# The inverse of the softmax sums sent over the partitions once per head group and applied as the context sums leave PSUM

## The reference, cut to what matters

```
xn = layernorm(ctx) * gamma_media + beta_media        # 722 media rows a batch
ln = layernorm(x + attn) * gamma_lat + beta_lat       # 100 latent rows
q  = (ln @ Wq + bq) * 128 ** -0.5                     # 8 heads of 128
k, v = split(concat([xn, ln]) @ Wkv + bkv)
out = softmax(q @ k.T) @ v                            # over 822 keys
x  = x + out @ Wo + bo
```

## Time and profile before

| | |
|---|---|
| median of three runs | 1082.91 us (1082.25 to 1085.74) |
| profiled execution | 1084.0 us, its span 1082.3 us |
| granted TensorE clock, mean | 0.975 of full speed |
| TensorE busy | 1011.3 us, 93% of the span |
| VectorE busy | 795.0 us, 73% |
| ScalarE busy | 580.2 us, 54% |
| GpSimd busy | 119.4 us, 11% |
| recurrence / units / last unit / tail / experts | 0 to 168 / 168 to 640 / 640 to 698 / 698 to 816 / 818 to 1082 us |

### The profile page before, as it was taken

One profiled execution on the slowest core, in us unless ns is written; L12 is line 12 of the kernel. 1 busy time (PEld: TensorE's weight loads), 2 busy tenths in 40 slices (PEclk: granted clock), 3 DMA queues, 4 the chain that ended last, 5 costly groups with the idle time before them and its releaser, 6 DMA issues.

```text
span 1082.3 us, 14817 instructions
## 1 busy us (share of the span) xinstructions
PE 1011.3 (93%) x5274; PEld 925.5 (86%) x5275; DVE 795.0 (73%) x1052; ACT 580.2 (54%) x770; POOL 119.4 (11%) x100
## 2 busy tenths in 40 slices
PE   8999998799999999999999997977798999999997
PEld 6969998798999999999999996966676888888886
DVE  6888456888878787888878655764567984956992
ACT  4426564545546464554646543641435864856881
POOL 3615001000000000000000000000012111111221
PEclk9999999899999999999999998998798999999999
DMA  9333877531525326252442138387555992975970
GB/s 262 124 109 125 304 266 243 129 114 47 167 79 138 131 61 177 66 168 75 132 141 47 61 48 279 109 262 260 125 163 158 344 364 68 353 251 176 363 285 22
DMA packets 119854, 183.88 MB, mean 170 GB/s; under 512 B 38945, under 2 KB 61985, under 8 KB 119795
## 3 DMA queue, kind: packets, MB, share of 16 engines
q1 hardware_dynamic: 118114, 178.55, 52.7%
q0 software_dynamic: 1680, 4.54, 1.2%
HBM read 146.94 MB, written 37.11 MB: 170 GB/s over the span
## 4 chain that ended last, share of the span: by engine, by line
PE 60%; DVE 15%; DMA 10%; ACT 6%; SPq 5%; issue 4%; POOL 0%; DVEq 0%; POOLq 0%; ACTq 0%
PE bank L587 17%; PE bank L588 16%; PE bank L589 16%; DMA xt_l<-scr_keys 4%; ACT xn_h L1457 2%; DVE z_l L1739 2%; DMA scr_rows<-mvr 2%; ACT z_h L1523 2%; PE bank L1334 2%; DVE str__65 L1721 1%; SPq L694 1%; PE bank L1072 1%; DMA w<-in_WoT 1%; PE bank L1074 1%; PE bank L1073 1%
## 5 line engine op out<-in xcount | busy, mean ns | idle before, releaser
L1739 DVE TENSOR_TENSOR wsl<-stage,wsh 128x2048 fp32r<-128x2048 f32 x63 | 143.7, 2291 | 23.1 <-ACT wsh L1528 18.1
L587 PE MATMUL bank<-ph,xn_h 128*128 128x400 f32 x384 | 140.2, 365 | 1.6 <-DVE pl L1739 1.6
L587 PE MATMUL bank<-qt_h,xt_h 128*128 128x400 f32 x384 | 134.8, 351 | 7.3 <-DMA xt_l<-scr_keys 7.3
L588 PE MATMUL bank<-pl,xn_h 128*128 128x400 f32 x384 | 133.3, 347 | 0.0
L588 PE MATMUL bank<-qt_l,xt_h 128*128 128x400 f32 x384 | 132.6, 345 | 0.0
L589 PE MATMUL bank<-ph,xn_l 128*128 128x400 f32 x384 | 132.5, 345 | 0.0
L589 PE MATMUL bank<-qt_h,xt_l 128*128 128x400 f32 x384 | 132.1, 344 | 0.0
L1528 ACT CAST wsh<-stage 128x2048 fp32r<-128x2048 f32 x63 | 120.4, 1918 | 10.6 <-PE bank L589 9.0
L1472 ACT ACTIVATE pa<-bank,rsr 128x400 f32<-128x400 f32 x96 | 56.4, 592 | 75.7 <-PE bank L589 72.3
L1498 ACT COPY zf<-bank 128x400 f32<-128x400 f32 x64 | 31.6, 494 | 101.7 <-PE bank L1190 101.4
L587 PEld LDWEIGHTS bank<-qt_h,xt_h 128*128 128x128 f32 x384 | 72.9, 190 | 9.0 <-issue 8.8
(11 more groups left out here) (277 smaller groups left out, 2330.3 us busy)
## 6 DMA issues: line engine op xcount, KB each, us to landing
stage<-in_W SPq DMA_DIRECT2D x63, 1024.0 KB, 6.1
scr_q<-st SPq DMA_DIRECT2D x16, 800.0 KB, 6.7
qf<-scr_q SPq DMA_DIRECT2D x16, 800.0 KB, 7.5
scr_z<-zf SPq DMA_DIRECT2D x16, 800.0 KB, 5.2
zr<-scr_z SPq DMA_DIRECT2D x16, 800.0 KB, 6.6
rt<-in_ctxT SPq DMA_DIRECT2D x7, 1444.0 KB, 13.2
raw<-in_ctx SPq DMA_DIRECT2D x8, 768.0 KB, 4.6
raw<-in_ctx SPq DMA_DIRECT2D x8, 512.0 KB
```

What stands on the lines that cost most here:

```text
L587: pe.matmul(dest, lh, rh, start=start and k == 0, stop=False)
L588: pe.matmul(dest, lh, rl, start=False, stop=False)
L1739: return dve.tensor_tensor(dst, src, high.bitcast(F32), ALU.subtract)
```

## The change

In place of dividing the heads' outputs in the tail, the context sums are divided as they leave PSUM:

- After each unit's reciprocal SyncE stores the 100x4 inverses to DRAM, waits for the landing, and loads them back as `inv`, 400 columns laid over the 128 partitions (`spread_inverse`, two DMAs per unit, one buffer).
- VectorE evacuates each context piece by a product with `inv` (`weighted`, 64 of them), ScalarE adds beta to it in place (`add_shift`, 64), which replaces `context_out`. The bank comes free after `weighted`.
- In the tail `ivt`, `cb`, `bmx`, `normalised` and the events `v` go. `V` has 400 columns; `ot_h` and `ot_l` read the bank.
- The first units' and the last unit's work is in another order on all engines, and SyncE issues the latent keys before the raw rows and the queries.

```
+            def spread_inverse(u):
+                b, g = divmod(u, 2)
+                sp.wait_ge(s_inv, u + 1)
+                sp.dma_start(d_iv[u].rearrange("(h t) -> t h", h=GH), iv[0:T, b, g * GH:(g + 1) * GH],
+                             allow_slow_non_contiguous=True).then_inc(s_ivd, 16)
+                sp.wait_ge(s_ivd, 16 * (u + 1))
+                sp.wait_ge(s_zn, ND * u)
+                sp.dma_start(inv[:], bc(d_iv[u], GR)).then_inc(s_ivl, 16)
...
+            def weighted(u, dc):
+                b, g = divmod(u, 2)
+                dve.wait_ge(s_zb, ND * u + dc + 1)
+                if dc == 0:
+                    dve.wait_ge(s_ivl, 16 * u + 16)
+                    if b:
+                        dve.wait_ge(s_zd[g], 16 * b)
+                dve.tensor_tensor(zf[g][:, :, dc, :], context_bank(u, dc)[:, 0:GR].rearrange("p (h t) -> p h t", h=GH),
+                                  inv[:].rearrange("p (h t) -> p h t", h=GH), ALU.mult).then_inc(s_zn, 1)
...
-                act.copy(zf[g][:, :, dc, :], zbank[n % 2][:, 0:GR].rearrange("p (h t) -> p h t", h=GH)).then_inc(s_zn, 1)
+            def add_shift(u, dc):
+                act.wait_ge(s_zn, ND * u + dc + 1)
+                at = zf[u % 2][:, :, dc, :]
+                act.activation(at, at, ACT.Identity, bias=gbm[:, 1, dc:dc + 1]).then_inc(s_zbeta, 1)
...
             def spread_sums(u):
-                pe.wait_ge(s_p, NP * (u + 1))
+                pe.wait_ge(s_sum, u + 1)
...
+            def context_bank(u, dc):
+                return bank[dc] if u == NU - 1 and dc >= 2 else zbank[dc % 2]
...
-                            pe.wait_ge(s_on, k - 3)
+                            pe.wait_ge(s_otl, ot_done(k - 4))
+                        elif k == 2:
+                            pe.wait_ge(s_zn, ND * NU)
...
                     elif what == "C":
+                        pe.wait_ge(s_zn, ND * NU)
...
-                        act.activation(ot_h[:, h, OVER:], ivt[k % NIV][:], ACT.Identity, bias=cb[:, h:h + 1]
+                        act.activation(ot_h[:, h, OVER:], bank[k % 4][:, 0:HT], ACT.Identity, bias=bv[:, h:h + 1]
...
-                    inverse(0)
+                    queries(1, 0)
                     for half in range(2):
                         keys_centred(1, half)
+                    inverse(0)
```

More of the change, by code:

```diff
@@ L221, in build @@
     x1b = [mem(f"x1b{k}", [P, D]) for k in range(2)]
-    dg = mem.over(x1b[0], "dg", [P, GR])
+    dg, inv = (mem.over(t, name, [P, GR]) for t, name in zip(x1b, ("dg", "inv")))
     tables_at = mem.where(pa[0]) + 4 * 4 * FC * 4
@@ L242, in build @@
     zn = HALF * ND * T
-    z_at = [(raw, 0), (raw, zn), (xt_h, HEADS * D + 64), (qt_h, -32), (xn_h, 2 * HEADS * HT - 32), (ph[0], 0)]
+    z_at = [(raw, 0), (raw, zn), (xt_h, HEADS * D + 64), (qt_h, 0), (xn_h, 2 * HEADS * HT), (ph[0], 0)]
     zr = [mem.over(t, f"zr{k}", [P, HALF, ND, T], skip=n) for k, (t, n) in enumerate(z_at)]
     z_l = [mem.over(t, f"z_l{k}", [P, HALF, ND, T], F32R, skip=n) for k, (t, n) in enumerate(z_at)]
[L246 to L252, removed]
+    z_h = [mem.over(qt_h, f"z_h{k}", [P, HALF, ND, T], F32R, skip=(k + 1) * zn) for k in range(3)]
+    z_h.append(mem.over(pa[0], "z_h3", [P, HALF, ND, T], F32R))
     UNITS = 2 * HEADS
@@ L266, in build @@
     ot_l = mem.over(xt_l, "ot_l", [P, HEADS, OVER + HT], F32R, skip=ot_skip + ot_n)
-    assert mem.where(xt_l) + ot_skip * 4 >= zr2_end + HT * 4
+    assert mem.where(xt_l) + ot_skip * 4 >= mem.where(xt_h) + (HEADS * D + 64 + HALF * ND * T) * 4
     mem.at = tail_at
@@ L1273, in _ @@
                 if u == 1:
+                    context(0, 0)
                     spread_sums(0)
-                if u < NU - 1:
+                    context(0, 1)
+                    turn_maxima(1)
+                    context(0, 2)
+                    spread_maxima(1)
+                    context(0, 3)
+                elif u < NU - 1:
                     context(u - 1, 0)
@@ L1279, in _ @@
                     spread_maxima(u)
+                    context(u - 1, 2)
+                    context(u - 1, 3)
                 else:
@@ L1282, in _ @@
                     context(u - 1, 1, lambda: spread_maxima(u))
-                context(u - 1, 2)
-                context(u - 1, 3)
+                    context(u - 1, 2)
+                    context(u - 1, 3)
             context(NU - 1, 0)
-            context(NU - 1, 1)
             spread_sums(NU - 1)
-            context(NU - 1, 2)
-            context(NU - 1, 3)
+            for dc in range(1, ND):
+                context(NU - 1, dc)
             finish(tail)
@@ L1608, in _ @@
                 if u == 1:
-                    evacuate(1, 0)
-                    queries(1, 0)
-                    for c in range(1, 5):
+                    for c in range(4):
                         evacuate(1, c)
@@ L2179, in _ @@
                     rows_norm(b + 1, 1)
-            weights(NU - 1)
-            values_low(3)
-            inverse(NU - 1)
+            u = NU - 1
+            shifts(u)
+            weighted(u - 1, 0)
+            for part in range(NP):
+                shift(u, part)
+            weighted(u - 1, 1)
+            first_sum(u)
+            weighted(u - 1, 2)
+            second_sum(u)
+            weights_low(u, 0)
+            weights_low(u, 1)
+            last_sum(u)
+            weights_low(u, 2)
+            weighted(u - 1, 3)
+            inverse(u)
+            for k in range(ND):
+                values_low(k)
             low_unit(0)
             low_unit(1)
+            weighted(u, 0)
+            weighted(u, 1)
             low_unit(2)
@@ L2187, in _ @@
             output_low(1)
+            weighted(u, 2)
             low_unit(3)
+            weighted(u, 3)
             output_low(2)
```

207 lines of the change are left out of this document (81 added, 126 removed), and 8 rows, old and new, of the table tail.

## The result

| | before | changed |
|---|---|---|
| median of the runs | 1082.58 us | 1133.43 us |
| profiled execution, span | 1082.3 us | 1130.1 us |
| granted TensorE clock, mean | 0.975 | 0.956 |

The ratio is 1.0484 (95% interval 1.0428 to 1.054): 4.8% slower. The direction was forecast, the size was not: 1096 us was predicted, and 1133 lies outside the 1080 to 1115 of the prediction's own case. (The kernel before has one more run here than in the table ahead of the prediction, hence 1082.58 for 1082.91.)

A forecast was written before the change was run, and what follows sets the result against it. TensorE was taken to bound the softmax units and a chain the tail, with a new DRAM round trip paid in each unit. 8 - 7 + 29 + 10 - 27 = +13 gave 1096 us, range 1064 to 1148.

The forecast's parts named there:

- the prediction's own case: Whole kernel: new store lands in 6.3 us, 1096 us in all, range 1080 to 1115; chance 0.42.
- Odd units: Six units, u = 3 to 13: `dg` 1.3 us late each, +8, less 7 for `xt_l`.
- a price per piece: New store of inverses: landing time above `rec`'s 2.7 us goes with the number of pieces, 400 against 768, giving 6.3 us.
- the -7 for `xt_l`: Odd units: latent keys put ahead of raw rows on SyncE remove TensorE's 7.3 us of waits for `xt_l`.
- Even units: Seven units, u = 2 to 14: spread 3.1 us late and 1.6 of clock, +29 in all; bounds 0 and +54.
- its idle fifth: VectorE over the units: 36 us of `weighted` products, 2.3 us a unit, fit its idle time and cost nothing.
- my two bounds: Even units: store lands at 501.3 if not hindered, 505.9 if it starts after the large transfers; middle 503.6 taken.
- First units: Piece 2 of unit 0's context waits 8.1 us for the inverse, 1.6 of clock: +10, bounds +6 and +13.
- Last unit: Unit 15 to `V` 1: earlier casts offset by waiting for `weighted(15,3)`, about 698 to 700; nothing counted.
- Tail: Heads follow every 2.6 us, then 2.4, where one took 4.68: -27, bounds -12 and -35.
- (b): Rival: the store doesn't get cheaper with fewer pieces, 9.6 us, 1153 us; 8 us gives 1125; chance 0.26.
- (a): Rival: adjacent elements cost nothing, the store lands in 2.7 us, 1061 us; chance 0.18.

The follow-up runs named there:

- e7: Kernel before with six test stores of inverses added, differing in number, size and spacing of pieces, each alone on the queue; ran once, 1093.35 us.
- e5: Kernel before with only SyncE's order changed, latent keys issued ahead of raw rows and queries; 1078.0 us, ratio 0.998 to the kernel before.
- e1: Changed kernel without the trip: no store or load of the inverses, `inv` set to one; 1108.9 us, ratio 1.025 to the kernel before.
- e2: Changed kernel with the inverses stored in 100 pieces of 16 bytes for 400 of 4, `inv` read with a stride; 1065.5 us, ratio 0.987.
- e4: Changed kernel with the raw rows issued ahead of the load of the inverses in odd units; 1194.2 us, ratio 1.105 to the kernel before.
- e3: Changed kernel, even units: store of the inverses issued ahead of `zf` and `qf`, load behind them; 1135.5 us, ratio 1.052 to the kernel before.
- e9: Changed kernel, 4-byte pieces, even units: whole trip (store, wait, load) made ahead of `zf` and `qf`; 1152.5 us, ratio 1.067.
- e16: e2 with VectorE's first product of each unit, `weighted(u-1,0)`, put behind the shifts; 1062.2 us, ratio 0.983 to the kernel before.
- e6: Kernel before with VectorE's three small beta operations moved behind the last low part of the weights; 1078.8 us, ratio 1.000.
- e13: Changed kernel without the trip: TensorE lays the sums over all partitions, VectorE takes the reciprocal of 128x400; 1084.3 us, ratio 1.003.

## Why the prediction was wrong

- **Odd units**, right in size: 5.8 us for the trip's store (6.3), `dg` 1.26 us late in u = 3 (1.3), 0.7 to 1.0 in the others, `xt_l` gone, -0.9 in all (+1). But the reason given for 6.3, a price per piece, is wrong: e7 shows one price for 100 to 800 neighbours, so that 6.3 came near 5.8 was luck. And the -7 for `xt_l` was counted without its price: by e5 the same order of SyncE's costs the even units 5.5 us.
- **Even units**, the step that failed: +68 and not +29. The step was "The reciprocal, 494.71 to 494.89, is just in time for that ... I take the middle, 503.6", with VectorE's products put at nothing ("which its idle fifth takes"). The parts, in u = 4 and counted from the unit's first score product:
  - The store goes out at 14.05 us, not 11.74 (+2.3), for the means' trip ends at 12.7, not at 8.8. I had left the means where they were. Their store goes out at +3.75; in the unit of the earlier trace rows it was at -1.15 (482.00 less 483.15). It is at +0.6 in e5, 1.65 in e1, 2.0 in e2. Taken in turn, that is an estimate of 1.8 us for the unit's earlier start without the wait for `xt_l`, some 1.2 for VectorE's products ahead of the statistics, and 1.7 for raw rows that are late behind the slow trip (e4, with the rows ahead, has 1.72).
  - The store lands after 11.7 us and not 8.7 (+3.0). The upper of my two bounds, a store that starts when the large transfers are done (11.0), was the right one; I took the middle. e3 and e9 show that what is beside it counts, ahead or behind.
  - The inverse takes 4.4 us from the landing to its use and not 3.6 (+0.8). That makes 6.1: the spread is 9.2 us later than before and not 3.1. The unit is 11.4 us longer than the one of the earlier trace rows; the 2.2 behind the spread, with the clock at 0.50, are put down to the clock (forecast 1.6).
  - Over all seven even units the trip is 48.6 of the 67.8 us; 19.2 stay without it (e1), and this the prediction had at nothing. 5.5 of them are SyncE's order, if what e5 shows in the kernel before holds here too; the rest is at least in part VectorE's 2.3 us of products a unit, which aren't hidden in its idle fifth where they stand ahead of `dg` (e16) and of the statistics.
- **First units**: +6.6 for +10. Piece 2 waits 9.49 us for the product (8.1 forecast), and two new waits of 3.56 (for `pl`) and 2.19 us (for the reciprocal, behind the centring) stand ahead of it; the one of 2.90 at 187.76 did go, and one of 5.87 for `pl`. The balance is +6.5. Of these five waits the sum had one.
- **Last unit**: +4.6 for 0. The last product is there at 63.7 us, not 58 to 60; its store took 11.1 us, beside the loads of `zr`. In e2, where that store takes 3.2 us, the stretch is 59.6 us.
- **Tail**: -30.0 for -27, right, and it holds in the other kernels with the change (55.2 to 57.0 us where it was 85.4). **Recurrence**: -4.2 for 0: I had looked at TensorE, which was busy, and not at VectorE; by e6 and the averages above some of it is beta, the rest is not told from the difference between executions.
- The rest, 3.8 us in the expert stage, is code that the change doesn't touch; e2's trace doesn't have it.
- Of the rivals, (b) came nearest in time (1153, and 1125 half way) and was half right: the price doesn't fall with the number, but it is 5.8 us and not 9.6. The fixed 2.0 us of the Trainium skill (DMA: Bandwidth & Descriptors, the anatomy of one DMA) doesn't hold for this store (5.8 alone); it is above what e7 has for the two other layouts of the same bytes, 1.33 and 1.75 us. Rival (a)'s 1061 us is nearly what the other layout gives, 1065.5 in e2, but (a) had adjacent elements cost nothing, and they do cost.

## What to carry to other kernels

Before a small tile goes through DRAM on the path of the busiest engine, look at how its pieces lie: one element per partition beside the next partition's cost 5.5 us a store and 11 beside traffic, four elements per partition 1.3 and 7. A transfer moved in a queue moves all that is behind it, and the one that had to stay early was not the new one. Work is hidden in an engine's idle share only if nothing that others wait for stands behind it.

## What the runs showed of the hardware

- A store of 100, 200, 400 or 800 neighbouring 4-byte pieces, each partition's beside the next one's, takes 5.2 to 6.0 us; 400 pieces 64 bytes apart 1.75, 100 of 16 bytes 1.33.
- With other transfers on the same queue such a store takes 6.9 to 8.3 us (361 KB just ahead, e9), 10.1 to 11.1 (1.6 MB behind as well, e3), 10.8 to 11.9 (1.6 MB ahead as well, changed kernel). The 16-byte one takes 7.0 behind 1.6 MB (e2).
- VectorE: a product of 128x400 with one operand in PSUM 571 ns, with the other operand read at a stride of 16 bytes 859 ns; a reciprocal of 128x400 from PSUM 2650 ns, 4.6 times a product (e13).
- Changed kernel: behind TensorE's wait of 6.39 us the granted clock is 0.50 and its matmuls of 400 columns take 0.54 us, the last at 340.62; behind the one of 1.26 us at 296.00 none of them takes 0.54.
